# First mixture of experts: result rows scattered to the tokens' places, clearings and row loads in another order

## The chip, the cores and the metric

The kernel runs on one core of one Trainium2 chip (trn2). The metric is device time in microseconds (us) for one execution of the whole program. The engines are named as in the profile: PE is TensorE, ACT is ScalarE, DVE is VectorE, POOL is GpSimd, SP is SyncE, and SPq is SP's DMA queue.

## What is computed

4096 tokens of 256 numbers (64 sequences of 64) pass through a first mixture of experts, a self-attention, a second attention with layer norms, and a second mixture of experts. The change is in the first mixture and at its border with the first attention. In the reference, cut to what matters:

```python
# first mixture: 8 experts of 256 -> 128 -> 256, each token takes the 2 best; 2 shared experts
logits = (x @ wt.T + repeat(g @ wg.T)) / 2
scores = softmax(logits)
topk_w, topk_idx = top_k(scores, 2);  topk_w = topk_w / topk_w.sum(-1)
gp = leaky(einsum('th,ehm->etm', x, w_gate)); up = einsum('th,ehm->etm', x, w_up)
y_all = einsum('etm,emh->eth', gp * up, w_down)
y = (y_all[topk_idx, arange(T)[:, None], :] * topk_w[..., None]).sum(1)
y = y + leaky(x @ sw_gate) * (x @ sw_up) @ sw_down
# then: x = x + attention1(y); x = x + second_mixture(attention2(x))
```

## The kernel before

The stages follow each other in one program. In the profiled execution the first mixture (`first_experts`) takes the time up to about 304 us, the first attention (`attention1`) that up to about 656 us, and the second mixture the time from about 1380 us to the end.

**Shared phase of the first mixture.** PE computes the two shared experts for 8 blocks of 512 tokens (NB = 8), each product as three matmuls of a high and a low part (L411, L412, L413). ACT and DVE make the high and low parts of everything. For each of the 10 experts (8 routed, 2 shared) SP loads the weights, ACT casts them to the high part (L563), and POOL subtracts to get the low part (L373, function `weights`). DVE also does the routing, in two halves (beta 0 and 1) of 16 tiles of 128 tokens. A half's routing gives each (token, choice) a slot in an array of 40 blocks of 128 slots, sorted by expert. Slots that no token takes have to be zero, so SP first writes 5 clearings of 1 MB over a half's slots (L296, `clear_slots`); both halves' are in SP's queue. POOL then copies the token rows to their slots, `x1_slots`, one indirect DMA for each tile and choice: 32 for a half (L380, `scatter`). In half 0 there are four scatters, then one subtraction, and so on, while the shared phase runs. In half 1 all 32 follow one after the other.

**Group loop.** A group is four blocks of slots, 10 groups to a half, 20 in all. In slot n of the loop PE transposes group n (L517), computes the first product of group n-1 (L411 to L413), transposes the hidden rows of group n-2 (L542) and computes the second product of group n-3. Every step hands over to ACT (L610 copies the transposed rows, L615 takes the gate product, L621 the hidden, L626 the result) and to DVE (L788, L794, L796, L801, L806). SP loads a group's rows (L342, two buffers) and stores its results, unweighted and in slot order, to `y1_slots` (L347).

**Way back.** POOL gathers each tile's two result rows from `y1_slots` with indirect DMAs (L402). DVE multiplies by the routing weights and adds (L713, L715: `scalar_tensor_tensor`). This happens for half 0 in the later part of the group loop. For half 1 the same is done inside the first attention: POOL gathers two rows' tiles in some of its slots (L935), and DVE adds (L1156, L1159). An attention slot is one tile of 128 tokens, 32 in all; in each, POOL subtracts the maxima (L914) and multiplies by the reciprocal sums (L920), PE makes the scores (L989) and DVE adds and reduces them (L1144, L1151, L1164). SP's queue in the first attention carries 40 clearings of 1 MB for the second mixture (L883, five for each block of four tiles) and the load of constants (`later.load`, in the block b = 2).

**Second mixture.** It has 80 groups of four blocks, and its results already go back by scatter. The place and the weight of a slot lie in the slot's tail, ACT (L2376) and DVE (L2429) scale a result of 128x256 on its way out of PSUM, and POOL scatters it to `y_rows`, four indirect DMAs for each group (L2296).

## Time and profile before

| | |
|---|---|
| time before, median of 3 runs (lowest to highest) | 1953.69 us (1950.52 to 1955.31) |
| profiled execution, its own time | 1956.01 us |
| its span, first to last instruction | 1954.3 us |
| busy: PE, PEld, DVE, ACT, POOL | 1444.0, 1127.3, 1133.9, 800.0, 967.9 us |
| mean granted TensorE clock, share of full speed | 0.893 |
| DMA, mean over the span | 143 GB/s, 278.87 MB |

No engine is busy all the time: PE has 74% of the span. A row of the profile names an engine, a line of the kernel, the operation and what it writes and reads; the bracket behind a row of a timeline is the idle time of that engine just before, and what ended it. "remote" there means that the profile does not see what released the wait.

### The profile page before, as it was taken

How to read it: one execution, taken by the hardware profiler on the slowest of the kernel's cores; microseconds unless marked ns; L12 is line 12 of the kernel's file. 1: busy time of each engine (PE TensorE's matmuls, PEld its weight loads, DVE VectorE, ACT ScalarE, POOL GpSimd, SP SyncE). 2: the span in 40 equal slices, each digit the busy share in tenths (PEclk: the TensorE clock that was granted, in tenths of full speed). 3: DMA queues.
4: the chain of work that ended last, by engine and by line, in shares of the span. 5: the costliest groups of instructions: out<-in, count | busy, mean ns of one | idle time of the engine just before them, and what ended most of it. 6: DMA issues, size and time to landing. Idle time of an engine off the chain costs nothing. (4 is left out here: it accounts for less than half of the span.)

```text
span 1954.3 us, 34466 instructions
## 1 busy us (share of the span) xinstructions
PE 1444.0 (74%) x11604; PEld 1127.3 (58%) x11605; DVE 1133.9 (58%) x2661; ACT 800.0 (41%) x1567; POOL 967.9 (50%) x888
## 2 busy tenths in 40 slices
PE   7945976576678799999999997520888867776771
PEld 4645973354445467776776765310777656666660
DVE  6634662578686546877777877540333355554545
ACT  2422431233344355556565654310443544444440
POOL 2471144666554211355555556553455565656662
PEclk9977987788789899999999998765988899999995
DMA  9553659356654000011111112637444577777755
GB/s 340 168 190 116 190 165 254 97 144 185 174 161 121 23 2 1 29 55 61 55 56 58 64 55 72 243 108 215 147 137 150 168 239 231 247 220 231 222 153 161
DMA packets 193490, 278.87 MB, mean 143 GB/s; under 512 B 27722, under 2 KB 161489, under 8 KB 190934
## 3 DMA queue, kind: packets, MB, share of 16 engines
q1 hardware_dynamic: 145030, 150.76, 26.3%
q0 software_dynamic: 33792, 84.23, 12.3%
q10 hardware_dynamic: 14544, 42.21, 7.3%
q8 instruction: 80, 1.31, 0.3%
q14 instruction: 44, 0.36, 0.1%
HBM read 133.38 MB, written 152.11 MB: 146 GB/s over the span
## 5 line engine op out<-in xcount | busy, mean ns | idle before, releaser
L2296 POOL DMA_INDIRECT y_rows<-se_ys,se_yidx x320 | 330.1, 1031 | 249.8 <-issue 209.5
L1461 POOL DMA_INDIRECT x_slots<-wide,a_sidx x256 | 258.8, 1011 | 101.1 <-issue 71.9
L2318 PE MATMUL ps<-ident,se_xs 128*128 128x128 f32 x640 | 94.6, 297 | 157.6 <-DMA se_xs<-x_slots 96.2
L1450 POOL TENSOR_TENSOR flat<-flat,a_rs 128x512 f32<-128x512 f32 x64 | 69.9, 1092 | 264.6 <-DVE a_rs L1943 264.6
L2329 PE MATMUL ps<-se_xsT,se_up 128*128 128x128 f32 x1280 | 177.7, 287 | 22.2 <-issue 21.5
L2420 DVE SCALAR_TENSOR_TENSOR se_hT<-ps,se_hT 128x512 f32<-128x512 f32 x80 | 55.2, 690 | 234.4 <-ACT se_hT L2370 181.6
L2341 PE MATMUL ps<-wide,se_hT 128*128 x640 | 168.0, 408 | 26.9 <-DVE se_hT L2420 13.0
L2318 PEld LDWEIGHTS ps<-ident,se_xs 128*128 128x128 f32 x640 | 80.4, 155 | 181.8 <-issue 159.0
L2329 PEld LDWEIGHTS ps<-se_xsT,se_up 128*128 128x128 f32 x1280 | 162.9, 201 | 29.2 <-issue 28.5
L2341 PEld LDWEIGHTS ps<-wide,se_hT 128*128 128x128 f32 x640 | 123.5, 203 | 49.2 <-issue 34.0
L2362 ACT COPY se_up<-w_up 128x256 f32 x320 | 106.2, 410 | 91.3 <-issue 89.9
L2370 ACT ACTIVATE se_hT<-ps 128x512 f32<-128x512 f32 x80 | 48.0, 600 | 231.7 <-remote 226.3
L1531 PE MATMUL ps<-w_up,flat 128*128 128x256 f32 x512 | 122.0, 393 | 13.5 <-ACT flat L1710 13.4
L1531 PEld LDWEIGHTS ps<-w_up,flat 128*128 128x128 f32 x512 | 100.0, 198 | 35.2 <-ACT flat L1710 15.3
L1571 PE MATMUL ps<-w_up 128*128 128x256 f32 x448 | 110.2, 395 | 9.6 <-ACT flat L1774 9.3
L914 POOL TENSOR_TENSOR flat<-flat,a_mx 128x1024 f32<-128x1024 f32 x32 | 60.9, 1903 | 103.8 <-DVE a_mx L1151 103.8
L969 PE MATMUL ps<-wide 128*128 128x512 f32 x128 | 77.6, 737 | 33.5 <-DVE wide L1131 30.7
L1571 PEld LDWEIGHTS ps<-w_up 128*128 128x128 f32 x448 | 83.7, 193 | 26.0 <-ACT flat L1774 10.8
L402 POOL DMA_INDIRECT wide<-y_slots,e_sidx1a x32 | 30.8, 963 | 107.0 <-DMA y_slots<-wide 76.7
L2429 DVE TENSOR_SCALAR se_ys<-ps,se_tail 128x256 f32<-128x256 f32 x160 | 69.6, 477 | 23.5 <-remote 8.8
L1144 DVE TENSOR_TENSOR flat<-ps,wide 128x1024 f32<-128x1024 f32 x32 | 39.2, 1225 | 70.6 <-PE ps L989 62.4
L2376 ACT ACTIVATE se_ys<-ps,se_tail 128x256 f32<-128x256 f32 x160 | 67.2, 476 | 21.5 <-remote 9.8
(339 smaller groups left out, 3524.0 us busy)
## 6 DMA issues: line engine op xcount, KB each, us to landing
x_slots<-wide SPq DMA_DIRECT2D x40, 1032.0 KB
se_xs<-x_slots SPq DMA_DIRECT2D x80, 516.0 KB
se_got<-y_rows ACTq DMA_DIRECT2D x64, 512.0 KB
x_slots<-wide SPq DMA_DIRECT2D x10, 1024.0 KB
wide<-x_slots SPq DMA_DIRECT2D x20, 512.0 KB
y_slots<-wide SPq DMA_DIRECT2D x20, 512.0 KB
w_up<-in_up SPq DMA_DIRECT2D x8, 1024.0 KB
y_rows<-se_ys,se_yidx POOLq DMA_INDIRECT x320
```

Of the source, the lines that this page charges most:

```text
L969: last = pe.matmul(ps[:, 1, :], w[:, c, m * P:(m + 1) * P], hT[:, c, :], start=(c == 0), stop=(c == C - 1))
L1450: pool.tensor_tensor(pn[:, m % 2].rearrange("p j h k -> p h j k"), sc[:, m % 2, :, :, 0:S], rs[:, m % 2].rearrange("p (h j) -> p h j", h=2 ...
L1461: pool.indirect_dma_start(out=x_slots, out_offset=bass.IndirectOffsetOnAxis(ap=sidx[:, r % 2, t, k_:k_ + 1], axis=0), in_=stage[:, t, k_, ...
L1531: last = pe.matmul(ps[:, 7, 0:D], oT[:, j, :], wo[:, j, :], start=(j == 0), stop=(j == J2 - 1))
L1571: last = pe.matmul(bank[:, a * 2 * P:(a + 1) * 2 * P], wq[:, c, (2 * jj + a) * P:(2 * jj + a + 1) * P], xT_[:, c, u * 2 * P:(u + 1) * 2 * ...
L2296: pool.indirect_dma_start(out=y_rows, out_offset=bass.IndirectOffsetOnAxis(ap=yidx[:, (w - 2) % TR, b:b + 1], axis=0), in_=ys[:, w % 2, b, ...
L2318: last = pe.transpose(ps[:, b // 2, (b % 2 * C + c) * P:(b % 2 * C + c + 1) * P], xs[:, w % XR, b, c * P:(c + 1) * P], ident[:])
L2329: last = pe.matmul(z_bank(w - 1)[:, b * P:(b + 1) * P], up[:, (w - 1) % 2, b, c, :], xsT[:, (w - 1) % 2, b, c, :], start=(c == 0), stop=(c ...
L2341: last = pe.matmul(y_bank(w, side)[:, (b % 2) * D:(b % 2 + 1) * D], hT[:, w % 2, b, :], w_dn[:, bass.ds(e[b], 1), :].rearrange("p o n -> p ...
L2362: last = act.copy(up[:, w % 2, b], w_up[:, bass.ds(e[b], 1)].rearrange("p o c m -> p (o c) m"))
L2376: last = act.activation(ys[:, w % 2, b, :], y_bank(w, 0)[:, b * D:(b + 1) * D], ACT.Copy, scale=tail[:, (w - 2) % TR, b, 1:2])
L2429: last = dve.tensor_scalar(ys[:, w % 2, b, :], y_bank(w, 1)[:, (b - 2) * D:(b - 1) * D], tail[:, (w - 2) % TR, b, 1:2], None, ALU.mult)
```

## The change

**Slots.** A row of `x1_slots` becomes 258 numbers wide. The last two are the place of the result among the half's 4096 result rows (2 x token + choice) and the routing weight. The clearings write a place that is out of range. The token rows are loaded twice (k = 0 and 1) into a buffer of 8 tiles, and POOL writes the two tail numbers into it by two small copies ahead of 8 scatters (`send`).

**Results.** Two DVE copies for each group take the places and weights out of the loaded slots (`tail_i`, `tail_w`). ACT and DVE each scale two results of 128x256 by the weight where they copied one of 128x512. POOL scatters a group's four results to `y1_rows`. The stores L347, the gathers L402 and L935 and the multiplication by weights in the additions are gone. The returned rows are loaded by plain DMAs: for half 0 in four loads' pairs, added by DVE in the last four slots of the group loop (128x1024), for half 1 in the first attention, two tiles a load, added in its slots 2 to 17.

**Order.** SP loads the weights of eight experts at the start, and POOL does all ten subtractions ahead of the first scatter. The five clearings of half 1 go from SP's queue to ACT's. The weights of routing are computed together with the slots. Five groups of slot rows may be loaded ahead. The constants' load in the first attention moves from block 2 to block 0, and the clearings there are 0, 6, 6, 6, 6, 6, 5, 5 to a block.

```diff
-                    def scatter(beta, t):
-                        if t % 8 == 0:
-                            pool.wait_ge(xr_in[t // 8], (beta + 1) * 16)
-                        for k in range(K1):
+                    def send(q):
+
+                        beta, mine = q // 4, slice(q % 2 * TPB, (q % 2 + 1) * TPB)
+                        pool.wait_ge(xr_in[q % 2], (q // 2 + 1) * K1 * 16)
+                        pool.tensor_copy(xr[:, mine, :, D:D + 1].bitcast(I32).rearrange("p t k o -> p t (k o)"),
+                                         ids1[:, q * TPB:(q + 1) * TPB, :])
+                        pool.tensor_copy(xr[:, mine, :, D + 1:ROW].rearrange("p t k o -> p t (k o)"),
+                                         wk1[beta][:, q % 4 * TPB:(q % 4 + 1) * TPB, :]).then_inc(tailed, 1)
+                        pool.wait_ge(tailed, q + 1)
...
-                    for w in range(2):
-                        pool.wait_ge(y1_out[w], GPB // 2 * 16)
-                    for t in range(TB):
-                        wait(pool, added1, t - 3)
-                        pool.nop(nofuse=True)
-                        for k in range(K1):
-                            pool.indirect_dma_start(
-                                out=got[:, t % 4, k, :], out_offset=None, in_=y1_slots[0],
+                    for g in range(NG1):
+                        pool.wait_ge(ya_done, NB + g + 1)
+                        pool.wait_ge(yb_done, g + 1)
+                        pool.nop(nofuse=True)
+                        for b in range(GB):
+                            pool.indirect_dma_start(
+                                out=y1_rows[g // GPB],
+                                out_offset=bass.IndirectOffsetOnAxis(ap=tail_i[:, g % TR1, b:b + 1], axis=0),
...
-                            wait(act, y1_out[g % 2], g // 2 * 16)
-                            act.copy(ys[:, g % 2, 0:2, :].rearrange("p b d -> p (b d)"), ps[:, 4, :]).then_inc(ya_done, 1)
+                            wait(act, y1_out[g % YR], returned(g % YR, g))
+                            for b in range(2):
+                                last = act.activation(ys[g % YR][:, b, :], ps[:, 4, b * D:(b + 1) * D], ACT.Copy,
+                                                      scale=tail_w[:, g % TR1, b:b + 1])
+                            last.then_inc(ya_done, 1)
...
+                        if b == 1:
+                            act.wait_ge(pad_step, 2)
+                            clear_slots(act, 1)
...
+                        if NG1 - 1 <= n:
+                            add_rows(n - (NG1 - 1))
...
-            GATHER_AT = [2 + j + j // TPB for j in range(TB)]
+            RETURNED_FROM = 2
+            FILLS = [0, 6, 6, 6, 6, 6, 5, 5]
...
+                    if b < 4:
+                        for w in range(2):
+                            sp.wait_ge(added1, 4 + max(0, 4 * b + 2 * w - 2))
+                            own = slice(b * TPB + 2 * w, b * TPB + 2 * w + 2)
+                            sp.dma_start(got[:, w], y1_tiles[1][:, own]).then_inc(got1_in[w], 16)
+                    if b == 0:
+                        later.load(sp)
```

GpSimd before, at the first subtractions (L373) and the row scatters of half 0 (L380).

```order
L373 TENSOR_TENSOR e_wl<-wide,e_wh 128x768 [waits e1_wh_ready] x2
L380 DMA x_slots<-e_xr,e_sidx1a 5120x256 [waits e1_xr_in0,e1_sidx_ready,padded]
L380 DMA x_slots<-e_xr,e_sidx1a 5120x256 x3
L373 TENSOR_TENSOR e_wl<-wide,e_wh 128x768 [waits e1_wh_ready]
L380 DMA x_slots<-e_xr,e_sidx1a 5120x256 x4
```

GpSimd in the changed kernel, the same place: the subtractions are L391, the two tail copies L397 and L399, the row scatters L405.

```order
L391 TENSOR_TENSOR e_wl<-wide,e_wh 128x768 [waits e1_wh_ready] x2
L391 TENSOR_TENSOR e_wl<-acc,e_wh 128x768 [waits e1_wh_ready] x6
L391 TENSOR_TENSOR e_wl<-wide,e_wh 128x768 [waits e1_wh_ready] x2
L397 COPY e_xr<-e_ids 128x8 [waits e1_xr_in0,e1_sidx_ready,padded]
L399 COPY e_xr<-e_wk1a 128x8
L405 DMA x_slots<-e_xr,e_sidx1a 5120x258 [waits e1_tailed]
L405 DMA x_slots<-e_xr,e_sidx1a 5120x258 x7
```

All ten subtractions now stand ahead of the first scatter, and the scatters are in runs of eight with two copies ahead of each run.

GpSimd before, from the last subtraction over half 1's scatters to the gathers of half 0 (L402).

```order
L373 TENSOR_TENSOR e_wl<-wide,e_wh 128x768 [waits e1_wh_ready]
L380 DMA x_slots<-e_xr,wide 5120x256 [waits e1_xr_in0,e1_sidx_ready,e1_pad1b]
L380 DMA x_slots<-e_xr,wide 5120x256 x15
L380 DMA x_slots<-e_xr,wide 5120x256 [waits e1_xr_in1]
L380 DMA x_slots<-e_xr,wide 5120x256 x15
L402 DMA wide<-y_slots,e_sidx1a 128x256 [waits y1_out0,y1_out1]
```

GpSimd in the changed kernel, from the last but one run of half 1 to the result scatters (L424).

```order
L405 DMA x_slots<-e_xr,e_sidx1b 5120x258 [waits e1_tailed]
L405 DMA x_slots<-e_xr,e_sidx1b 5120x258 x7
L397 COPY e_xr<-e_ids 128x8 [waits e1_xr_in1]
L399 COPY e_xr<-e_wk1b 128x8
L405 DMA x_slots<-e_xr,e_sidx1b 5120x258 [waits e1_tailed]
L405 DMA x_slots<-e_xr,e_sidx1b 5120x258 x7
L418 CAST wide<-pad_i 128x1 [waits e1_made]
L424 DMA y_rows<-wide,e_tail_i 4096x256 [waits e1_ya_done,e1_yb_done]
L424 DMA y_rows<-wide,e_tail_i 4096x256 x3
```

Half 1's run of 32 is cut into four of eight, and behind it stand four scatters for each group of the loop in place of the gathers.

ScalarE before, around the shared phase's blocks b = 1 and b = 2 (L590 takes the gate product, L578 the block's result, L569 the next features).

```order
L590 ACTIVATE wide<-ps 128x512 [waits e1_h_ready,e1_z_ps] x2
L578 COPY acc<-ps 128x1024 [waits e1_y_ps]
L596 CAST e_hh<-wide 128x512 [waits e1_y_ps,e1_h_ready] x2
L569 CAST e_xh<-wide 128x1024 [waits e1_z_ps]
L563 CAST e_wh<-wide 128x768 [waits e1_weights0]
L590 ACTIVATE wide<-ps 128x512 [waits e1_h_ready,e1_z_ps] x2
L578 COPY acc<-ps 128x1024 [waits e1_y_ps]
```

The same place in the changed kernel (now L628, L612, L634 and L601; L288 is the clearing).

```order
L628 ACTIVATE wide<-ps 128x512 [waits e1_h_ready,e1_z_ps] x2
L612 COPY acc<-ps 128x1024 [waits e1_y_ps]
L634 CAST e_hh<-wide 128x512 [waits e1_y_ps,e1_h_ready] x2
L601 CAST e_xh<-wide 128x1024 [waits e1_z_ps]
L288 DMA x_slots<-wide 128x8x258 [waits pad_step]
L288 DMA x_slots<-wide 128x8x258 x4
L628 ACTIVATE wide<-ps 128x512 [waits e1_h_ready,e1_z_ps] x2
```

The five clearings of half 1 now stand in ACT's stream behind block 1's features and ahead of block 2's gate products.

## Rows read from the trace of the kernel before

**Rows 1.** Busy time by stretch, numbers of instructions, granted clock, DMA share, GB/s

```profile
core 0: us, PE busy (x) PEld busy (x) DVE busy (x) ACT busy (x) POOL busy (x), PEclk, DMA share, GB/s
118.00:163.00 45.00, 8.07 (x48) 7.47 (x48) 2.45 (x2) 2.02 (x2) 31.12 (x33) 0.60 0.55 187
...
235.00:304.70 69.70, 49.99 (x343) 46.22 (x342) 41.20 (x69) 18.57 (x30) 30.80 (x33) 0.83 0.54 166
```

**Rows 2.** Waits between 110 and 180 us, in total, times, longest

```profile
ACT wide L615 <- remote: 25.2, 1, 25.2
```

**Rows 3.** Timeline of TensorE around the wait (start, us, engine, line, operation)

```profile
130.33 1.97 PE L517 MATMUL ps<-ident,wide 128*128 128x128 f32 x8 [13.48 <-DMA wide<-x_slots]
...
139.77 0.28 PE L413 MATMUL ps<-e_wh,e_xl 128*128 x1
139.89 1.04 PE L517 MATMUL ps<-ident,wide 128*128 128x128 f32 x8
```

**Rows 4.** Timeline of GpSimd, subtractions and row scatters of the first mixture

```profile
116.51 1.81 POOL L373 TENSOR_TENSOR e_wl<-wide,e_wh 128x768 fp32r<-128x768 f32 x1
118.49 0.99 POOL L380 DMA_INDIRECT x_slots<-e_xr,wide  x1 [0.17 <-issue]
...
157.78 0.96 POOL L380 DMA_INDIRECT x_slots<-e_xr,wide  x1 [0.30 <-issue]
```

**Rows 5.** Timeline of ScalarE, group loop of the first mixture

```profile
163.04 0.60 ACT L615 ACTIVATE wide<-ps 128x512 f32<-128x512 f32 x1 [25.23 <-remote]
...
186.55 0.60 ACT L615 ACTIVATE wide<-ps 128x512 f32<-128x512 f32 x1 [1.86 <-PE ps L413]
...
237.29 0.60 ACT L615 ACTIVATE wide<-ps 128x512 f32<-128x512 f32 x1 [1.86 <-PE ps L413]
...
242.65 0.59 ACT L626 COPY wide<-ps 128x512 f32<-128x512 f32 x1 [4.28 <-remote]
...
300.42 0.59 ACT L626 COPY wide<-ps 128x512 f32<-128x512 f32 x1 [3.21 <-PE ps L413]
```

**Rows 6.** Timeline of GpSimd in the second mixture, bursts of eight result scatters

```profile
1502.95 0.98 POOL L2296 DMA_INDIRECT y_rows<-se_ys,se_yidx  x1 [3.72 <-issue]
...
1511.99 0.99 POOL L2296 DMA_INDIRECT y_rows<-se_ys,se_yidx  x1 [0.31 <-issue]
...
1529.62 0.98 POOL L2296 DMA_INDIRECT y_rows<-se_ys,se_yidx  x1 [3.30 <-issue]
```

**Rows 7.** Timeline of ScalarE in the second mixture, after such a burst

```profile
1513.79 0.60 ACT L2370 ACTIVATE se_hT<-ps 128x512 f32<-128x512 f32 x1 [6.36 <-remote]
```

**Rows 8.** Costliest groups of the page, result row scaled on ScalarE

```profile
L2376 ACT ACTIVATE se_ys<-ps,se_tail 128x256 f32<-128x256 f32 x160 | 67.2, 476 | 21.5 <-remote 9.8
```

**Rows 9.** Timeline of SyncE's queue, clearings into an idle and into a busy queue

```profile
11.11 14.16 SPq L296 DMA_DIRECT2D x_slots<-wide  x5
...
396.12 10.97 SPq L883 DMA_DIRECT2D x_slots<-wide  x5
```

**Rows 10.** Timeline of ScalarE in the shared phase, block b = 2

```profile
60.32 0.60 ACT L590 ACTIVATE wide<-ps 128x512 f32<-128x512 f32 x1 [4.50 <-PE ps L413]
```

**Rows 11.** Timeline of VectorE, routing's end and a pair beside GpSimd's subtraction

```profile
102.74 1.33 DVE L694 TENSOR_SCALAR wide<-wide 128x32 int32<-128x32 f32 x1
103.98 1.28 DVE L749 TENSOR_TENSOR e_hl<-wide,e_hh 128x512 fp32r<-128x512 f32 x2
...
110.05 2.27 DVE L749 TENSOR_TENSOR e_hl<-wide,e_hh 128x512 fp32r<-128x512 f32 x2 [2.14 <-issue]
```

**Rows 12.** Waits between 352 and 385 us, in attention

```profile
DVE acc L1156 <- DMA w_up<-y_slots,wide: 10.5, 1, 10.5
```

**Rows 13.** VectorE by line from 305 to 656 us, the two additions of a tile

```profile
L1159 DVE SCALAR_TENSOR_TENSOR acc<-w_up,wide,acc 128x256 f32<-128x256 f32 x16 | 29.0, 1815 | 0.6
L1156 DVE SCALAR_TENSOR_TENSOR acc<-w_up,wide,acc 128x256 f32<-128x256 f32 x16 | 17.3, 1079 | 10.5 <-DMA w_up<-y_slots,wide 10.5
```

**Rows 14.** Timeline of GpSimd, start of the first attention

```profile
304.70 0.11 POOL L888 MEMSET a_own<- 128x8 f32 x1 [8.16 <-POOLq L188]
```

More of the change, by code:

```diff
@@ L581, in _ @@
                     features(0)
-                    features(1)
                     weights(0)
                     weights(1)
+                    features(1)
+                    for q in range(2, 6):
+                        weights(q)
                     exponential(0)
+                    weights(6)
+                    weights(7)
                     for b in range(NB):
@@ L946, in slot @@
                         normalize(n - 1)
-                    if n in GATHER_AT:
-                        gather(GATHER_AT.index(n))
                     if n == TPB:
```

346 lines of the change are left out of this document (185 added, 161 removed).

## The prediction

> **What bounds the kernel now.** I read the busy times by stretch first, to see where the engines that the change touches leave each other idle. Between 118 and 163 us PE is busy for 8.07 of 45 us, at a granted clock of 0.60, while POOL is busy for 31.12; between 235 and 304.7 us PE is busy for 49.99 of 69.7 and POOL for 30.80 [rows 1]. Both are stretches in which POOL issues indirect DMAs. So I read the waits there. One wait carries the first: ACT L615 waits 25.2 us on "remote" [rows 2]. PE's timeline tells what it waits for. PE had finished the product that L615 reads at 140.05 (139.77 + 0.28) and stopped after the next transposes at 140.93; ACT starts at 163.04 [rows 3, 5]. The data was there and the signal was not. What else ran is POOL's run of half 1's scatters, 118.49 to 158.74 [rows 4]. I read it so: inside a long unbroken run of indirect DMAs, PE's signals get stuck after some work (here 16 transposes and the 24 product matmuls whose signal is the stuck one), and come free a little after the run ends, here 4.3 us.
>
> Two other places show the same thing smaller. In the second mixture, POOL's result scatters come in runs of eight, and ACT L2370 starts at 1513.79 after a "remote" wait of 6.36 us, 0.8 us after such a run ended at 1512.98 [rows 6, 7]. In the group loop, the clean pitch is 5.64 us: ten L615 rows from 186.55 to 237.29 make nine intervals. With gathers running, the first ACT row after them has a "remote" wait of 4.28 us. From 237.29 (group 13) to the last result at 300.42 are eight slots, 63.13 us, or 7.9 us each [rows 5]. The bound of the loop is PE's slot as long as POOL is quiet, and the signals when it is not.
>
> The Trainium skill, page "SBUF — State Buffer", section "SBUF: two separate sides", says that only DVE and GpSimd share a port pair and that PE and ACT never wait on anyone. By that rule alone there would be no hold, and the loop's pitch would stay at PE's; its sum would be that of the first rival below. The rows above speak against it for signals, with 25.2 us.
>
> **The change part by part.** I follow the time from the start. Signs are against before; minus is faster.
>
> (1) Shared phase. ACT gets five clearings ahead of block 2's gate products. Issuing five costs the queue 10.97 us when it was idle before and 14.16 us among other loads [rows 9]. I take 11. In the same block before, ACT idles 4.50 us for PE ahead of its second L590, so that much is cover [rows 10]: about +7. Below this the bound is 0, if ACT's issue is fast and PE's buffers cover it; above it is +14. The clearings leave SP, which only brings the other loads forward.
>
> (2) Subtractions and sends of half 0. The ten subtractions are the same work, pulled ahead. They run beside DVE's routing. A pair of L749 takes 2.27 us beside a subtraction and 1.28 without [rows 11], 1 us more, so eight subtractions cost DVE some 8 us at most, mostly off the path as DVE idles between its pairs. The 32 scatters then come in four runs of eight, 10.1 us a run (8 x 1.27, from 31 intervals between 118.49 and 157.78 [rows 4]), where before they stood in fours. Between runs are two copies of 128x8 and two waits, some 1 us. Here is the doubtful step. Runs of eight do hold PE's signals in the second mixture, fours do not visibly do so in the shared phase. I take 1.3 us of delay for each of the four runs, +5. The bounds are 0 and, if the copies don't break the run, a stall like the 25.2 us one [rows 2]. The shared phase would then end some 12 us later than before, near 130 us.
>
> (3) Hold at the start of the group loop. Half 1's 32 scatters need the routing, which ends at 104.07 us before (102.74 + 1.33 [rows 11]), now some 10 us later with the weights in it; the run starts at about 122 against 118.49. With four small breaks it takes 42 us and ends at 164 against 158.74, and the signals come free at 168 against 163. But each break lets PE through once, so I count that groups are two slots further at that moment: 163.04 was group 0's gate product, now it is group 2's. 168 - 2 x 5.64 = 156.7, so this is -6 against 163. The bounds: no break counts (+5), or each two runs give two slots (-17).
>
> (4) Loop with result scatters. Group 0's gate product at 163.04 to the last result at 300.42 is 21 slots in 137.4 us before [rows 5]. Now 19 slots remain from 168. POOL has 4 x 1.29 = 5.2 us of scatters in each slot, of a slot that PE could do in 5.64. That is nearly an unbroken run. The nearest row is the second mixture, which has the same scheme: runs of two groups each begin at 1502.95 and, two runs on, at 1529.62, so four groups take 26.67 us, or 6.67 a group [rows 6]. 19 x 6.7 = 127, so the last result leaves at 295 against 300.42. The bounds are 5.64 (no hold) and 7.9 (as with the gathers): -20 and +23 around this value. ACT's results are two of 0.476 us in place of one of 0.59 [rows 8, 5], and DVE's likewise, both with idle time in each slot; two small tail copies of DVE are hidden the same way. The stores and their 20 waits on SP disappear, hidden before and after.
>
> (5) The border. Before, the attention's first POOL instruction starts at 304.70, 4.3 us behind the last result [rows 14, 5]. Now four scatters (5.2 us) and a landing of 2 to 4 us follow the last result: 295 + 8 = 303. I take -3 for the sum of (1) to (5) rather than -2 to -5.
>
> (6) Attention. The DVE wait of 10.5 us on a gather's landing [rows 12] goes: the rows come by SP's plain loads, and the first two are ahead of the constants that are the likely reason for it. The second addition of a tile takes 1.815 us on average and the first 1.079 [rows 13]; both are the same work, so at least 0.74 us a tile is waiting beside POOL's work and its gathers. 16 x 0.74 = 12, and as DVE is not the bound in each slot I take 8. Together -18.5. The bounds: the stall reappears as a wait on the constants, which nothing in the first slots needs (-8), or all of the additions' waiting goes and PE's signals are never late (-30). Larger clearings a block (six for five) are on a queue that has room.
>
> **Sum.** -3 - 18.5 = -21.5 against the profiled execution of 1956.0 gives 1934.5. The median of the runs shown is 2.3 lower than that execution, so I forecast 1932 us.
>
> **The rivals.**
> First, no hold any more: runs broken every eight scatters or four never catch PE. For it speaks that fours in the shared phase show none. Against it are the waits behind runs of eight [rows 6, 7] and behind the gathers [rows 5]. Then (1) to (3) end at about 147 (130, plus load, transposes and product) for group 0's gate product, and 21 slots of 5.64 follow: last result at 265, which is 35 us earlier. With the attention's -18.5 that makes 1953.7 - 35 - 18.5 = 1900. With the pitch alone at 5.64 it is 1932 - 20 = 1912.
>
> Second, what is gained in attention is spent in the loop: a pitch of 7.9. Then 1932 + 23 = 1955, no change.
>
> Third, the slower side: half 0's four runs are one run for PE. It would start at about 48 us, when the subtractions are through, and last 42 us, with the shared phase in it. The 25 us wait comes a second time, in the place of the 5 us of term (2), and half 1's run is not broken either, so term (3) is +5 and not -6. 1932 + 20 + 11 = 1963; where the stall is as long as the run less the 11 us before it catches, 31 us, it is 1969. It decides from the point where more than some 22 us of shared phase are lost. For it: the copies between are as short as the pause of 0.30 us between scatters is, within a factor of three. Against it: the pause of 3.3 us between runs of eight is enough [rows 6], and a subtraction of 1.81 us between runs of four was enough [rows 4]; 1 us lies below both.
>
> **Chances.** Forecast, pitch 6.3 to 7.2: 0.45, own range 1922 to 1944. First rival: 0.19, 1893 to 1918. Second: 0.14, about 1950 to 1958. Third: 0.22, 1958 to 1975. The range that leaves a tenth out on either side is 1898 to 1969. Within 0.3% (5.9 us, about what a measurement of this kernel can tell) is 1948 to 1960. Faster 0.64, same 0.15, slower 0.21.
>
> **What would show it.** Right: ACT's clearings (L288) as one block of about 11 us before block 2's gate products; POOL's L405 in fours of eight runs with PE's loop a few slots on at the end; L424 in runs of four or eight with pauses of 1 to 3 us and a "remote" wait of ACT behind them; no DVE wait over 2 us on returned rows. Wrong: PE idle for 20 us or more between 50 and 100 us (third rival); a pitch of 5.6 beside the L424 rows (first); ACT waiting on the result buffers' scatters to land, which would be a wait that I have at nothing.

## The result and the profile after

The changed kernel takes 1976.91 us (median of 4 runs, 1972.39 to 1990.86), the kernel before 1954.5 us (4 runs). The ratio is 1.0126, with a 95% interval of 1.0071 to 1.0182: the change makes this kernel slower, by 22 us between the medians. The forecast was 1932 us, faster; the time lies above the range's end of 1969.

First the changed kernel's ScalarE timeline, the rows that answer to [rows 5] and [rows 10]: a wait for weights, the clearings in ACT's queue (ACTq), the last shared block's copy, the first gate product (L656), the last result (L668) and the attention's first row (L1119).

```profile
45.61 1.56 ACT L595 CAST e_wh<-wide 128x768 fp32r<-128x768 f32 x2 [9.53 <-DMA wide<-in_w1down]
...
50.49 4.07 ACTq L288 DMA_DIRECT2D x_slots<-wide  x2
...
54.59 17.00 ACTq L288 DMA_DIRECT2D x_slots<-wide  x3
71.69 0.60 ACT L628 ACTIVATE wide<-ps 128x512 f32<-128x512 f32 x1 [19.64 <-issue]
...
141.12 1.01 ACT L612 COPY acc<-ps 128x1024 f32<-128x1024 f32 x1 [7.02 <-remote]
...
175.19 0.60 ACT L656 ACTIVATE wide<-ps 128x512 f32<-128x512 f32 x1 [23.11 <-remote]
...
326.46 0.84 ACT L668 ACTIVATE wide<-ps,e_tail_w 128x256 f32<-128x256 f32 x2 [2.63 <-PE ps L436]
346.94 0.59 ACT L1119 COPY wide<-ps 128x512 f32<-128x512 f32 x1 [19.63 <-PE ps L1013]
```

The five clearings take ACT's queue from 50.49 to 71.59 us, and block 2's gate products start at 71.69. The last shared block is taken out at 141.12 (116.88 before). The first gate product comes at 175.19 (163.04 before, [rows 5]) after a "remote" wait of 23.11, the last result at 326.46 (300.42 before).

GpSimd's timeline of the changed kernel, the rows that answer to [rows 4] and [rows 14]: the break between two runs of row scatters, then the last result scatters (L424) and the attention's start.

```profile
161.39 0.21 POOL L397 COPY e_xr<-e_ids 128x8 int32<-128x8 int32 x1
...
162.48 0.98 POOL L405 DMA_INDIRECT x_slots<-e_xr,e_sidx1b  x1 [0.76 <-POOL e_xr L399]
...
314.87 1.18 POOL L424 DMA_INDIRECT y_rows<-wide,e_tail_i  x1 [5.82 <-DVE wide L854]
...
322.35 1.18 POOL L424 DMA_INDIRECT y_rows<-wide,e_tail_i  x1 [2.44 <-DVE wide L854]
...
337.27 0.98 POOL L424 DMA_INDIRECT y_rows<-wide,e_tail_i  x1 [0.30 <-issue]
345.77 0.10 POOL L948 MEMSET a_own<- 128x8 f32 x1 [7.52 <-POOLq L191]
```

Between two runs of eight there are 0.2 us copies and about 1 us of break. At the end, POOL scatters from 322.35 to 338.25 without a pause, up to 12 us beyond the last result, and the attention's first instruction comes 7.52 us behind that, at 345.77 (304.70 before, there 8.16 us behind the last gather).

Busy time by stretch, as in [rows 1], and a wait of the first mixture, as in [rows 2] but from 0 to 345 us:

```profile
118.00:163.00 45.00, 25.04 (x148) 22.45 (x146) 17.44 (x56) 8.93 (x12) 25.92 (x33) 0.80 0.56 180
235.00:304.70 69.70, 59.62 (x454) 57.06 (x454) 37.84 (x75) 25.62 (x46) 35.96 (x37) 0.93 0.47 146
```

```profile
ACT wide L656 <- remote: 46.8, 6, 23.1
```

PE does more in these two stretches than before (25.04 for 8.07, 59.62 for 49.99) since the loop's work comes later, not since it is faster.

The first instruction of the second attention on POOL, in the kernel before and in the changed one, marks the end of the first attention:

```profile
661.11 1.04 POOL L1450 TENSOR_TENSOR flat<-flat,a_rs 128x512 f32<-128x512 f32 x1 [10.80 <-DVE a_rs L1943]
```

```profile
684.79 1.04 POOL L1498 TENSOR_TENSOR flat<-flat,a_rs 128x512 f32<-128x512 f32 x1 [10.80 <-DVE a_rs L1991]
```

So the difference builds up like this, in us from the start of the span. The last three columns belong to two runs further down.

| point | before | changed | difference | f1 (before) | f2 (changed) | difference |
|---|---|---|---|---|---|---|
| last shared block taken out by ACT | 116.88 | 141.12 | +24.2 | 114.07 | 134.34 | +20.3 |
| first gate product (ACT) | 163.04 | 175.19 | +12.2 | 138.01 | 141.85 | +3.8 |
| last result (ACT) | 300.42 | 326.46 | +26.0 | 253.54 | 262.28 | +8.7 |
| attention starts (POOL) | 304.70 | 345.77 | +41.1 | 263.93 | 281.62 | +17.7 |
| second attention starts (POOL) | 661.11 | 684.79 | +23.7 | 613.12 | 619.72 | +6.6 |
| span | 1954.3 | 1976.9 | +22.6 | 1770.3 | 1774.0 | +3.7 |

The first mixture loses 41 us in three parts (12.2 by the loop's first gate product, 13.9 in the loop, 15.0 behind it), and the first attention gives back 17.4. The attention's two additions of a tile, to be read against [rows 13], by line:

```profile
L1208 DVE TENSOR_TENSOR acc<-acc,w_up 128x256 f32<-128x256 f32 x16 | 32.1, 2006 | 0.6
L1206 DVE TENSOR_TENSOR acc<-acc,w_up 128x256 f32<-128x256 f32 x16 | 15.3, 954 | 0.0
```

They are no cheaper than before. What is gone is the 10.5 us wait of [rows 12], and with it every "remote" wait of this stage: the kernel before has three lines with such waits in the first attention, 13.1, 7.3 and 2.0 us in all (L1099, L1144, L1070), the changed one has none.

### The profile page after: what moved, and what is told of

It is laid out like the page before. It is cut to its first block and busy times, and to the rows that moved or that the text cites. A ratio compares the mean times of both kernels' runs of the same rounds, so it can differ in the third digit from the quotient of the medians.

```text
span 1976.9 us, 34732 instructions
## 1 busy us (share of the span) xinstructions
PE 1461.3 (74%) x11604; PEld 1141.3 (58%) x11605; DVE 1138.0 (58%) x2705; ACT 803.2 (41%) x1587; POOL 985.8 (50%) x922
## 3 DMA queue, kind: packets, MB, share of 16 engines
q0 software_dynamic: 34560, 84.30, 12.2%
## 5 line engine op out<-in xcount | busy, mean ns | idle before, releaser
L2344 POOL DMA_INDIRECT y_rows<-se_ys,se_yidx x320 | 325.5, 1017 | 260.1 <-issue 221.9
L2377 PEld LDWEIGHTS ps<-se_xsT,se_up 128*128 128x128 f32 x1280 | 165.0, 203 | 42.8 <-issue 40.0
L2389 PE MATMUL ps<-wide,se_hT 128*128 x640 | 168.8, 411 | 23.7 <-issue 8.2
L424 POOL DMA_INDIRECT y_rows<-wide,e_tail_i x80 | 79.7, 997 | 86.0 <-DVE wide L854 61.8
L434 PE MATMUL ps<-e_wh,e_xh 128*128 x160 | 52.7, 330 | 35.9 <-DVE wide L842 33.2
L1990 DVE TENSOR_REDUCE a_rs<-flat 128x8 f32<-128x520 f32 x64 | 44.4, 694 | 52.9 <-ACT flat L1747 51.0
```

The lines of the kernel that those rows point to most:

```text
L424: pool.indirect_dma_start(out=y1_rows[g // GPB], out_offset=bass.IndirectOffsetOnAxis(ap=tail_i[:, g % TR1, b:b + 1], axis=0), in_=ys[g % ...
L2344: pool.indirect_dma_start(out=y_rows, out_offset=bass.IndirectOffsetOnAxis(ap=yidx[:, (w - 2) % TR, b:b + 1], axis=0), in_=ys[:, w % 2, b, ...
L2377: last = pe.matmul(z_bank(w - 1)[:, b * P:(b + 1) * P], up[:, (w - 1) % 2, b, c, :], xsT[:, (w - 1) % 2, b, c, :], start=(c == 0), stop=(c ...
L2389: last = pe.matmul(y_bank(w, side)[:, (b % 2) * D:(b % 2 + 1) * D], hT[:, w % 2, b, :], w_dn[:, bass.ds(e[b], 1), :].rearrange("p o n -> p ...
```

## The experiments

The runs were measured in five sets, each on one chip and with the kernel before beside it: e1 to e4 on chip 4, e5 to e8 on chip 6, e9 to e11 on chip 1, f1 to f4 on chip 2, g1 to g3 on chip 1. In the first two sets the kernel before takes 1958 and 1959 us. Times of different sets are compared by their ratios to it, and each trace is of one execution.

**e1: the clearings of half 1 back on SP.**

```diff
+                    clear_slots(sp, 1)
                     load_rows(2)
...
-                        if b == 1:
-                            act.wait_ge(pad_step, 2)
-                            clear_slots(act, 1)
```

> The changed kernel with one edit undone: the five clearings of half 1 are issued by SP again, between the features' load and the row loads, and not by ACT. Theory A (ACT's queue is what makes the shared phase late): ACT's wait of 19.6 us ahead of block 2's gate products goes, the last shared block is taken out some 15 to 20 us earlier than at 141.1, half 1's first row scatter starts near 112 instead of 129.6, and the time falls by 10 to 17 us, to a ratio near 1.005 of the kernel before. Theory B (the sends in runs of eight and the late row loads make it late): the clearings now delay the row loads on SP, the scatters of half 0 end later, and the time moves by less than 5 us.

Measured: 1969.52 us, ratio 1.006 (1.0027 to 1.0092). ScalarE's timeline of this run, the same kinds of rows as above:

```profile
46.67 1.56 ACT L596 CAST e_wh<-wide 128x768 fp32r<-128x768 f32 x2 [10.05 <-DMA wide<-in_w1down]
...
62.83 1.01 ACT L613 COPY acc<-ps 128x1024 f32<-128x1024 f32 x1 [4.66 <-remote]
...
100.05 1.01 ACT L613 COPY acc<-ps 128x1024 f32<-128x1024 f32 x1 [5.85 <-remote]
...
139.06 1.01 ACT L613 COPY acc<-ps 128x1024 f32<-128x1024 f32 x1 [7.08 <-PE ps L437]
...
162.65 0.60 ACT L654 ACTIVATE wide<-ps 128x512 f32<-128x512 f32 x1 [13.29 <-remote]
```

ACT's 19.6 us standstill is gone, but the shared phase ends at 139.06, 2 us earlier only. With ACT free, remote waits of 4.66 and 5.85 us stand ahead of the blocks' copies while half 0's scatters run, and the wait for weights is 10 us as before. For the shared phase theory B is right: the two delays don't add, each hides the other. The time is another matter: the ratio falls from 1.0126 to 1.006, which is what theory A asked for, and the trace is 8 us shorter (1968.5 for 1976.9). That gain comes from the first gate product, 162.65 for 175.19: this time the signal came free before the last run of scatters was over, after 13.29 us. The third run had ended at 158.00, and the break behind it was 2.5 us and not 1, as POOL waited for its rows.

**e2: the kernel before with the attention's new order on SP.**

```diff
-                    if b == 2:
-                        later.load(sp)
...
-                    for g in range(b * fills, (b + 1) * fills):
+                    if b == 0:
+                        later.load(sp)
+                    for g in range(filled, filled + FILLS[b]):
```

> The kernel before with only the order of SP's queue in the first attention as in the change: the constants are loaded in block 0 and the clearings are 0, 6, 6, 6, 6, 6, 5, 5 to a block. Theory A (the attention's gain of 19 us is half the gather's late landing beside the constants, half the end of gathers): the wait of 10.5 us goes and the time falls by 8 to 11 us, to a ratio near 0.995. Theory B (the gain is that no gathers are left, and the constants have no part in it): the wait on the gather only moves to another tile, and the ratio stays within 0.998 and 1.002.

Measured: 1948.49 us, ratio 0.996 (0.9932 to 0.9988). VectorE by line, as in [rows 13]:

```profile
L1161 DVE SCALAR_TENSOR_TENSOR acc<-w_up,wide,acc 128x256 f32<-128x256 f32 x16 | 30.6, 1910 | 0.6
L1158 DVE SCALAR_TENSOR_TENSOR acc<-w_up,wide,acc 128x256 f32<-128x256 f32 x16 | 17.7, 1105 | 0.0
```

The wait on a gather is gone (it was behind L1158's counterpart), the additions are as long as before. Theory A by the median: the order alone is worth about 8 us (0.004 of 1955), with all gathers still there, though the interval, 2 to 13 us, also touches theory B's 0.998. The trace, of an execution of 1954.96 us, shows less. The first attention takes 352.3 us in it (308.70 to 660.97), 4.1 less than before, and the "remote" waits of the stage are still there:

```profile
ACT wide L1101 <- remote: 13.0, 4, 3.7
DVE flat L1146 <- remote: 7.0, 2, 3.8
```

```profile
660.97 1.04 POOL L1452 TENSOR_TENSOR flat<-flat,a_rs 128x512 f32<-128x512 f32 x1 [10.80 <-DVE a_rs L1945]
```

So the changed kernel's gain of 17.4 us in this stage is not all the order's: by these traces 13 us of it come with the end of the gathers and of these waits.

**e3: the changed kernel without result scatters.** SP stores each group's results in slot order, and the later loads take the first 4096 rows, so results reach the wrong tokens; the gathering is left out.

```diff
+                    def store_slots(g):
+                        sp.wait_ge(ya_done, NB + g + 1)
+                        sp.wait_ge(yb_done, g + 1)
+                        sp.dma_start(yv[g // GPB][g % GPB], ys[g % YR]).then_inc(y1_out[g % YR], 16)
...
-                    for g in range(NG1):
-                        pool.wait_ge(ya_done, NB + g + 1)
...
```

> The changed kernel with the 80 result scatters of the first mixture left out: SP stores each group's results in slot order instead, and the later loads take the first 4096 rows of that, so the results reach the wrong tokens. All else is as in the change. Theory A (the scatters hold PE's signals, and their backlog stands at the end): the loop's pitch falls from 7.2 us to near 5.7, 21 slots take 119 to 122 us instead of 151.3, the attention's first GpSimd instruction comes 4 to 6 us behind the last result instead of 19.3, and the time falls by 40 to 46 us, to a ratio near 0.99. Theory B (the slots are long since ACT and DVE scale the results and copy the tails): the pitch stays over 6.5, and only the 14 us at the end go.

Measured: 1938.08 us, ratio 0.99 (0.9868 to 0.9932). ScalarE's timeline, gate products, the last result and the attention's first row:

```profile
181.46 0.60 ACT L660 ACTIVATE wide<-ps 128x512 f32<-128x512 f32 x1 [22.42 <-remote]
...
229.06 0.60 ACT L660 ACTIVATE wide<-ps 128x512 f32<-128x512 f32 x1 [1.85 <-PE ps L440]
...
299.49 0.84 ACT L672 ACTIVATE wide<-ps,e_tail_w 128x256 f32<-128x256 f32 x2 [2.65 <-PE ps L440]
310.25 0.59 ACT L1123 COPY wide<-ps 128x512 f32<-128x512 f32 x1 [9.92 <-PE ps L1017]
```

21 slots take 118.0 us (299.49 - 181.46), 5.62 each, although ACT and DVE still scale the results and copy the tails. The attention's first ACT row follows after 9.92 us, not 19.63. Theory A: the scatters cost the loop 33 us against this run (151.3 - 118.0) and some 10 us behind it. The edit changes nothing ahead of the loop, and the wait ahead of the first gate product is there (22.42).

**e4: the kernel before with half 1's clearings on ACT.**

```diff
-                    clear_slots(1)
...
+                        if b == 1:
+                            act.wait_ge(pad_step, 1)
...
+                            for g in range(EB // 8):
+                                act.dma_start(slots[g],
+                                              pad_row[:, 0:D].unsqueeze(1).to_broadcast([P, 8, D])).then_inc(pad1[1], 16)
```

> The kernel before with only the five clearings of half 1 taken from SP's queue and issued by ACT behind block 1. Theory A (the issue of a clearing takes as long as the DMA queues are full, whoever issues it): ACT stands still for 12 to 20 us, the last shared block ends 8 to 14 us later than at 117.9, and the time rises by 5 to 12 us. Theory B (the 21 us in the changed kernel came from its own other loads, the queue of the kernel before is free at that time): ACT stands for about 11 us, of which PE hides 4 to 5, and the time rises by less than 4 us, as the stall that ends at 163 hides it.

Measured: 1968.82 us, ratio 1.005 (1.0026 to 1.0073). ScalarE's timeline and its queue:

```profile
43.52 1.29 ACTq L605 DMA_DIRECT2D x_slots<-wide  x2
44.83 2.92 ACTq L605 DMA_DIRECT2D x_slots<-wide  x1
47.78 8.14 ACTq L605 DMA_DIRECT2D x_slots<-wide  x2
56.02 1.09 ACT L589 ACTIVATE wide<-ps 128x512 f32<-128x512 f32 x2 [10.21 <-issue]
...
171.72 0.60 ACT L620 ACTIVATE wide<-ps 128x512 f32<-128x512 f32 x1 [25.14 <-remote]
```

The queue takes 12 us here (43.52 to 55.92) and 21 in the changed kernel, and ACT stands still for 10.21 us: of the length theory B was right. The last shared block is taken out at 125.54, 8.7 us late, and the first gate product comes at 171.72, as much later. Nothing hid it: the stall's end moves with the scatters. Of the time theory A is right, 10 us more.

**e5: the kernel before with pauses in half 1's scatters.** GpSimd multiplies the next two tiles in place by 1.0, three times, each waited for, behind each fourth scatter.

```diff
+                        if beta and t % 2 == 0 and t:
...
+                            for i in range(3):
+                                own = xr[:, t:t + 2, :].rearrange("p t d -> p (t d)")
+                                pool.tensor_scalar(own, own, 1.0, None, ALU.mult).then_inc(made, 1)
+                                pauses += 1
+                                pool.wait_ge(made, pauses)
```

> The kernel before with half 1's 32 row scatters cut into eight runs of four: ahead of each run but the first, GpSimd multiplies the next two tiles in place by 1.0, three times, each waited for (about 2 us). Theory A (what holds PE's signals is the unbroken run of indirect DMAs, and a pause of 2 us sets it free): ACT's wait of 25.2 us on the first gate product falls below 8 us, several groups of half 0 are through when the scatters end near 172, and the time falls by 8 to 16 us. Theory B (the signals come only when all the scatters are through, pauses or not, as the changed kernel's breaks of 1 us did nothing from 151.6 to 172.3): ACT's first gate product comes near 176 and the time rises by 8 to 12 us.

Measured: 1950.37 us, ratio 0.9963 (0.9943 to 0.9984). GpSimd's and ScalarE's timelines:

```profile
130.40 1.03 POOL L389 DMA_INDIRECT x_slots<-e_xr,wide  x1 [0.76 <-POOL e_xr L384]
...
135.28 4.67 POOL L384 TENSOR_SCALAR e_xr<-e_xr 128x512 f32<-128x512 f32 x3
140.71 1.03 POOL L389 DMA_INDIRECT x_slots<-e_xr,wide  x1 [0.76 <-POOL e_xr L384]
```

```profile
141.30 0.60 ACT L624 ACTIVATE wide<-ps 128x512 f32<-128x512 f32 x1 [2.33 <-PE ps L422]
...
146.77 0.60 ACT L624 ACTIVATE wide<-ps 128x512 f32<-128x512 f32 x1 [3.59 <-PE ps L422]
```

The pauses are longer than meant, 5.4 us, so that the last scatter is at 196.07. Still the first gate product is taken at 141.30, 2.33 us after the wait began, in place of 163.04, and the next slot follows in 5.5 us. Breaking up the run, and nothing else, removed the 25 us wait. This shows that the unbroken run of indirect DMAs holds the signal; theory A, whose 8 to 16 us are met at their lower end (9 us between the medians). Such signals, that reach ACT or DVE long after PE is done, are called late signals below. Smaller ones stay: a remote wait of 3.78 us at 177.41, between two pauses, and some of up to 10 us beside the later gathers.

**e6: the changed kernel with a pause in the middle of each of half 1's runs.** The same kind of pause, with two multiplications, in the middle of each run of eight.

```diff
+                            if beta and t == 2:
...
+                                for i in range(2):
+                                    own = xr[:, q % 2 * TPB + 2:q % 2 * TPB + 4, :, 0:D].rearrange("p t k d -> p (t k) d")
+                                    pool.tensor_scalar(own, own, 1.0, None, ALU.mult).then_inc(made, 1)
+                                    pauses += 1
+                                    pool.wait_ge(made, pauses)
```

> The changed kernel with a pause of about 2 us in the middle of each of half 1's four runs of eight row scatters (GpSimd multiplies the two tiles that are sent next by 1.0 in place, twice), so there are runs of four with breaks of 2 and 1 us in turn. Theory A: the wait of 23.1 us ahead of the first gate product falls below 10 us, and the time falls by 8 to 15 us although the scatters take 8 us longer. Theory B: the wait lasts to the last scatter, near 183, and the time rises by 6 to 10 us.

Measured: 1980.68 us, ratio 1.0111 (1.007 to 1.0152), so the time is neither theory's. The first gate product came at 159.56, with 2.76 us of waiting on PE, so the signal was free, as theory A has it. But no time was gained:

```profile
205.96 1.00 POOL L433 DMA_INDIRECT y_rows<-wide,e_tail_i  x1 [0.16 <-issue]
```

The first result scatter stands in POOL's queue behind all of half 1's row scatters, here at 205.96, where the changed kernel has it at 192.04. There are three buffers for results, so the loop can't be further ahead than that. A part of the 14 us is the pauses' own: they came out at over 6 us each in place of 2 (a pair of multiplications takes 5.7). I had missed POOL's order in the first rival too: an early start is worth little while it is this one.

**e7: ACT's casts of the last two experts behind block 1's gate products**, and **e8: e7 and e1 together.**

```diff
+                        if b == 1:
+                            weights(8)
+                            weights(9)
                         if b:
                             take_shared(b - 1)
...
-                        if b == 0:
-                            weights(8)
-                            weights(9)
```

> The changed kernel with ACT's casts of the last two experts moved behind block 1's gate products, so that ACT doesn't wait 9.5 us for their weights ahead of those. Theory A (that wait is the first 7 us of the shared phase's 24): block 0's result is taken out near 42 instead of 48.0, block 1's near 66 instead of 72.7. Whether the total follows depends on the routing of half 1: it should move half 1's scatters, and the total, by 4 to 7 us. Theory B (the clearings in ACT's queue are issued only when the DMA queues are empty enough, at a fixed time near 71): block 1's result stays at 72 to 73 and the total within 2 us.

> Both edits: the clearings of half 1 by SP, and the casts of the last two experts behind block 1's gate products. Theory A (two waits of ACT explain the shared phase, the sends' share is small): the last shared block is taken out at 122 to 128, and the time lies 10 to 16 us below the changed kernel's. Theory B (with ACT free, the sends in runs of eight catch the shared phase, as in the run that only moved the clearings): it is taken out at 132 or later, with remote waits of 4 to 6 us at ACT, and the time is less than 10 us below the changed kernel's.

e7 measured 1973.73 us, ratio 1.008 (1.0048 to 1.0111), and its trace has the last shared block at 146.74, later than the changed kernel's. The queue of ScalarE:

```profile
47.14 9.76 ACTq L288 DMA_DIRECT2D x_slots<-wide  x1
...
56.93 20.41 ACTq L288 DMA_DIRECT2D x_slots<-wide  x2
77.44 1.09 ACT L628 ACTIVATE wide<-ps 128x512 f32<-128x512 f32 x2 [27.16 <-issue]
```

Asked for 4 us earlier, the clearings take 31 us and let ACT go at 77.44. The casts' place alone frees nothing, which theory B had; that the stall grows as the clearings are asked for earlier, neither theory had. What made it longer the runs don't show. e8 measured 1957.15 us, ratio 0.9996 (0.9971 to 1.0022), with the last shared block at 128.85, the first gate product at 148.29 and the attention's start at 324.26. Its trace is 20 us shorter than the changed kernel's, and e7, of the same set, is 17 us slower: more than theory A asked for (10 to 16), though the shared block is 1 us later than its bound. In this set the change with two repairs costs and gains nothing; the loop still takes 156.6 us for 21 slots and 19.4 us follow it.

**e9, e11, e10: short pauses.** e9 is e5 with one multiplication (1.5 us, 2.3 us between runs) and e2's order; e11 is e9 with pauses behind every eighth scatter only; e10 is e8 with one such multiplication in the middle of each run of half 1. The edits against e5's lines, and for e10 against e6's:

```diff
-                            for i in range(3):
+                            for i in range(1):
...
-                        if beta and t % 2 == 0 and t:
+                        if beta and t % 4 == 0 and t:
...
-                                for i in range(2):
+                                for i in range(1):
```

> The kernel before with SP's order of the changed kernel in the first attention, and with half 1's 32 row scatters cut into eight runs of four by shorter pauses than in the first run with pauses: one multiplication in place by 1.0 instead of three (1.6 us, with the wait some 2.3 us between runs). Theory A (a pause of 2.3 us behind four scatters sets PE's signals free as one of 5.4 us did, and the order's gain of 8 us adds to it): the first gate product comes near 141 and the ratio to the kernel before is 0.988 to 0.992. Theory B (it takes a pause as long as the signals are late, 4 to 5 us): ACT has remote waits of over 8 us between 141 and 180 and the ratio is 0.994 to 0.998, the order's gain alone.

> As the run with short pauses and the attention's order, but with a pause only behind each eighth row scatter of half 1, so runs of eight as in the changed kernel with breaks of some 2.3 us instead of 1. Theory A (the length of the run counts: within eight scatters the signals get stuck): ACT has two or more remote waits of 4 to 10 us between 141 and 170, and the ratio lies 0.002 to 0.005 above that of the run with pauses behind every fourth. Theory B (only the break's length counts, and 2.3 us is enough): no difference to it beyond 0.001.

> The changed kernel with three edits: the clearings of half 1 by SP, the casts of the last two experts behind block 1's gate products, and one pause of about 3.5 us in the middle of each of half 1's four runs of eight row scatters. Theory A (the hold at the loop's start is the third part of the loss): the first gate product comes near 140 instead of 148.3, and the time falls by 3 to 8 us below the run with the first two edits, to a ratio of 0.995 to 0.998 of the kernel before. Theory B (from here on the loop is bound by the result scatters and their backlog at its end, so an earlier start only makes the scatters wait for each other): within 2 us of the run with the two edits.

Measured: e9 1754.65 us, ratio 0.9929 (0.9902 to 0.9956); e11 1757.94, 0.9944 (0.9923 to 0.9965); e10 1775.34, 1.0039 (1.002 to 1.0057). The kernel before took 1768.11 us in this set. No trace of the three has a remote wait of ACT in the first mixture, so they tell nothing of pauses and signals, and all three lie outside the ranges of their theories. e10 still tells of POOL's order: its loop starts at 138.88 and its last result comes at 263.92, 3 us earlier and 1.6 us later than in the changed kernel of f2 below.

**f1, f2: the kernel before and the changed kernel once more**, with e9 and e11 again (f3, f4) and with e9, e11 and e10 a third time (g1, g2, g3).

> The kernel before, unchanged, for a trace of it on the chip of this call. Theory A (late signals are the chip's property): where the time is near 1955 us, ACT's first gate product waits over 20 us on remote; where it is near 1768 us, it comes within 4 us of PE's product, near 141, and the ratio is 1 in either case. Theory B (they were an accident of single profiles): the trace has them or not regardless of the time.

> The changed kernel, unchanged. Theory A (its loss is the shared phase's delay by ACT's queue and the result scatters' backlog, late signals only add to it): where signals are late the ratio is 1.010 to 1.014; where none is late it is still above 1, between 1.003 and 1.012, with the loop's pitch at 5.7 to 6.2 us. Theory B (its loss is all late signals): where none is late the ratio is below 0.995.

The kernel before took 1769.4 and 1770.7 us in these two sets. f1: 1769.07, ratio 0.9998 (0.9976 to 1.0021). f2: 1776.93, ratio 1.0053 (1.0027 to 1.0079). ScalarE's timeline of f1 and a row of its page, to be read against [rows 5]:

```profile
138.01 0.60 ACT L615 ACTIVATE wide<-ps 128x512 f32<-128x512 f32 x1 [3.49 <-PE ps L413]
...
253.54 0.59 ACT L626 COPY wide<-ps 128x512 f32<-128x512 f32 x1 [2.11 <-PE ps L413]
```

```profile
L2370 ACT ACTIVATE se_hT<-ps 128x512 f32<-128x512 f32 x80 | 47.8, 597 | 58.0 <-PE ps L2329 56.3
```

The same program, and the 25.2 us wait is 3.49 us; the whole trace of f1 has no "remote" wait, nor has that of f2. Half 1's 32 scatters run without a break as before. ACT's L2370 in the second mixture idles 58.0 us in all, on PE, where the page of the kernel before, taken ahead of all these sets, has 231.7, of which 226.3 remote. ScalarE's timeline of f2:

```profile
54.11 15.31 ACTq L288 DMA_DIRECT2D x_slots<-wide  x3
69.53 1.09 ACT L628 ACTIVATE wide<-ps 128x512 f32<-128x512 f32 x2 [17.82 <-issue]
...
141.85 0.60 ACT L656 ACTIVATE wide<-ps 128x512 f32<-128x512 f32 x1 [1.85 <-PE ps L436]
...
262.28 0.84 ACT L668 ACTIVATE wide<-ps,e_tail_w 128x256 f32<-128x256 f32 x2 [2.67 <-PE ps L436]
282.78 0.59 ACT L1119 COPY wide<-ps 128x512 f32<-128x512 f32 x1 [19.66 <-PE ps L1013]
```

Without late signals the changed kernel's slot is 5.73 us (120.4 / 21) with all result scatters in it, against 5.50 in f1 (115.5 / 21). It still loses: the clearings hold ACT for 19 us, though of the 20.3 us by which the shared phase is late only 3.8 are left at the loop's start, and the attention waits 19.66 us for the scatters' backlog, its first POOL instruction 19.3 us behind the last result in place of 10.4. This is the right half of the table above. Theory A for f1 and f2.

f3 and f4 gave 0.9945 (0.9919 to 0.997) and 0.9948 (0.9924 to 0.9972), g1 and g2 0.9905 (0.9872 to 0.9938) and 0.9931 (0.9905 to 0.9957), g3 1.0038 (1.0013 to 1.0062). For runs without late signals f3, f4 and g3 came as expected (0.990 to 0.996, within 0.001 of f3, 1.002 to 1.006); g1 was expected at 0.992 to 0.996 and g2 within 0.001 of it, and both missed by about 0.0015, less than their intervals. e9's kernel is faster than the kernel before in each of its three sets, by 0.6 to 1%, and pauses behind every fourth or every eighth scatter can't be told apart (0.0003 to 0.0026, with intervals of 0.002 to 0.003). How much the pauses give is open: there is no set in which they met late signals. The changed kernel with both repairs and pauses (e10, g3) stays 0.4% above the kernel before, where it has 0.5% without them (f2): without late signals the repairs bring back little.

## Why the prediction was wrong, step by step

The attention was to start at 303 and started at 345.77, 42.8 us later; the attention itself came out near its term. The 42.8 us add up so: the stuck signal came free at 175.19 and not at 168, +7.2, terms (1) and (2); the two slots that the breaks were to give did not come, 2 x 7.2 = +14.4, term (3); the other 19 slots were 0.5 us longer each, +9.9, term (4); the border took 19.3 us and not 8, +11.3, term (5).

**What bounds the kernel.** The reading that a long run of indirect DMAs holds PE's signals is shown by e5 and e3, for the conditions of the first two sets. f1 shows that it isn't a property of the program alone. The Trainium skill ("SBUF — State Buffer", "SBUF: two separate sides") says of the engines' ports that only the pair shared by DVE and GpSimd makes an engine wait, and that PE and ACT never wait on anyone. f1 and f2, with no remote wait, agree with that; the wait of 25.2 us is one for a signal, and whether a port had a part in it no run shows.

**(1) Shared phase, ACT's clearings: +7 forecast, the step that failed first.** The term of the sum was sized from an idle and a lightly loaded queue (11 to 14 us [rows 9]). It measured 21.1 us of the queue and 19.64 of ACT's standstill, less the 4.50 of cover +15, where the range had +14 as its bound. The kernel before's ACT needs 12 for as many clearings (e4), and its SP took 13 for those of half 1:

```profile
35.56 13.07 SPq L296 DMA_DIRECT2D x_slots<-wide  x5
```

So the row at nearly the same moment of the program would have given +9 and not +15. What makes the rest is not shown. In the changed kernel the twice loaded token rows, the features and, from 51.26 on, half 0's row scatters are issued around the clearings, and 14.4 MB are moved between 30 and 80 us where e4 moves 12.0.

**(2) Subtractions and sends.** "The same work, pulled ahead" left out that the last two experts' weights come behind half 0's clearings. ACT stands 9.53 us for them ahead of block 1, and block 0 is taken out 6.9 us late. The runs of eight cost about twice the +5 where ACT is free to feel it: e1's remote waits of 4.66 and 5.85 add up to 10.5, and e8's shared phase ends at 128.85 where e10's, with the same order and no late signals, ends at 118.29. The forecast also took runs of four as harmless, and they are not quite: e2, e4 and e5 have remote waits of 4.13, 3.94 and 3.89 us in the shared phase. Together the phase ended 24 us late, not 12.

**(3) Loop's start: -6 forecast, +12.2 measured.** The breaks of 1 us did not let PE through twice. PE had finished the first group's product at 153.00, one break fell between that and the last scatter (161.39 to 162.48), and the signal came only at 175.19, 2.9 us behind the last scatter. For the forecast it would have had to be group 2's.

**(4) Loop: a pitch of 6.7 forecast, 7.2 measured (151.3 / 21), over 21 slots and not 19.** The mechanism was right (e3) and the size near; the second mixture's rows were a fair guide. The error here is 10 us from the pitch and 14 from the two slots that (3) had promised.

**(5) Border: 8 us behind the last result forecast, 19.3 measured.** In the last slots PE has fewer groups in flight, so the results of the last three groups come at 320 to 326.5, faster than POOL's 5.2 us a group. I priced four scatters (5.2 us) and a landing of 2 to 4. From 322.35 on twelve went out in one run, eight of them behind the last result, which is 11.8 us, and the landing was 7.52; [rows 14] had 8.16 for it. The attention waits for them (ACT L1119, 19.63 us).

**(6) Attention: -18.5 forecast, -17.4 measured.** The size was right, but of its two parts only one: the sum came out by luck. The wait of 10.5 us went, and it belonged to the order of SP's queue: in e2 it is gone with all gathers in place. The 8 us for the additions did not come, they are as long as before. In their place the 22.4 us of remote waits went, which I had put into the bound only ("PE's signals are never late"): e2, with the order alone, still has 20 of them and needs 352.3 us, the changed kernel 339.0. Where no signal is late, the attention gains 11.1 us (338.1 for 349.2), and e9, with gathers and the new order, takes 337.7 us for the same stretch. There the whole gain is the order's.

**The rivals.** The third one's sign and time (1963 to 1969, own range to 1975) were nearest, its cause was not: half 0's runs never held PE for 20 us. The longest idle time of PE between 50 and 100 us is 11.7, ahead of 73.79, and ends with ACT's standstill. What I had not weighed is that ACT's queue and POOL's queue each got work in an order that stops the loop ahead and behind.

## What to carry to other kernels

Five clearings of 1 MB took the queue of their issuing engine 11 to 31 us here, depending on the moment: read the price from a row at the same moment of the program, take its spread as the bound, and don't put bulk clearings in the stream of an engine that computes. When results leave by scatter instead of by store and gather, count what is still in the scattering queue when the last result is there, since that queue's backlog is at the end of the stage, where nothing covers it. Change an order by itself before the mechanism that comes with it: here the order of one queue was worth about 8 us, and the rest of the change lost some 30 us in the same conditions (22 in all, with the order's 8 in it; an estimate from two sets).

## What the runs showed of the hardware

The same kernel, unchanged, took 1954 to 1959 us in the first measurements and 1768 to 1771 us in the later ones. The difference goes with the late signals: 226.3 us of remote waits at one line of the second mixture in the one, none in the other, and 25.2 against 3.5 us at the loop's start. That line's idle time alone, 231.7 against 58.0 us, is 174 of the 184 us between the two traces. The long times are those of chips 4 and 6, the short ones those of chips 1 (twice) and 2. That fits a difference between chips, but no chip was measured in both conditions, and the long ones all came first, so the cause stays open. Where signals were late, a pause of 5.4 us behind four indirect DMAs set the first gate product's signal free; a break of 1.1 us behind eight did not, and behind one of 2.5 us it came 4.7 us after the last DMA of the run (e1).
